# Laying out weights and adapter tables on the host, in a fused four-layer kernel on one Trainium2 core

## The reference, cut to what matters

```
x: [128, 64, 1024] f32
x = x + ssm(x)                      # causal convolution per channel, masked by length, kernel from 64 modes
x = x + einsum('bct,bcd->bdt', x, L1_weights[cond])
x = x + x @ W2.T + bias + (x @ A2[id].T) @ B2[id].T       # W2 [1024,1024], A2 [32,16,1024], B2 [32,1024,16]
x = x + x @ W3.T + 0.5 * (x @ A3[lab]) @ B3.T             # W3 [1024,1024], A3 [5,1024,32], B3 [1024,32]
```

## Time and profile before

| | us |
|---|---|
| median of three runs | 1587.73 |
| lowest, highest | 1584.13, 1589.02 |
| profiled execution, its time | 1586.82 |
| its span, first to last instruction | 1585.1 |
| TensorE busy | 1533.4 (97%) |
| VectorE, ScalarE, GpSimd busy | 992.8, 612.8, 390.3 |

### The profile page before, as it was taken

The page is one execution under the profiler, slowest core; times in us unless marked ns, Lnnn a source line. Parts: engine busy times, 40 slices in busy tenths (PEclk is TensorE's granted clock), DMA queues, the critical chain, the costliest instruction groups (busy, mean ns, idle before and its releaser), DMA issues.

```text
span 1585.1 us, 33854 instructions
## 1 busy us (share of the span) xinstructions
PE 1533.4 (97%) x11213; PEld 1478.3 (93%) x11213; DVE 992.8 (63%) x2010; ACT 612.8 (39%) x1185; POOL 390.3 (25%) x389
## 2 busy tenths in 40 slices
PE   6899989999999999599999999999999999999998
PEld 5778879999999999599999999999999999999998
DVE  7955358888888888545556556455564555655544
ACT  3331245444445545234434334343333433434432
POOL 3551246666666666200000000000000000000000
PEclk9999999999999999699999999999999999999999
DMA  9723156676666666443443534435345353353442
GB/s 242 105 105 102 41 174 235 234 241 234 233 238 238 236 235 218 118 123 107 143 136 101 159 111 138 140 93 166 113 126 149 97 153 125 109 156 106 143 135 73
DMA packets 165103, 243.02 MB, mean 153 GB/s; under 512 B 62113, under 2 KB 118701, under 8 KB 162417
## 3 DMA queue, kind: packets, MB, share of 16 engines
q1 hardware_dynamic: 154844, 208.11, 44.2%
q10 hardware_dynamic: 10230, 34.52, 6.2%
HBM read 167.62 MB, written 74.95 MB: 153 GB/s over the span
## 4 chain that ended last, share of the span: by engine, by line
PE 58%; issue 0%; ACT 0%; DVE 0%; DMA 0%; DVEq 0%
PE ps L1531 23%; PE ps L1532 22%; PE ps L1502 7%; PE ps L1539 2%; PE ps L1541 2%; PE ps L1513 1%; PE ps L1508 0%; DMA x_in<-x_d 0%; ACT a L1303 0%; DVE weights L1399 0%; ACT xa L1305 0%; ACT weights L1315 0%; DVE y_out L1480 0%; ACT xs L1320 0%; DVE y_out L1483 0%
## 5 line engine op out<-in xcount | busy, mean ns | idle before, releaser
L1531 PE MATMUL ps<-weights,xs 128*128 128x256 f32 x1536 | 398.2, 289 | 0.0
L1532 PE MATMUL ps<-weights,xs 128*128 128x256 f32 (+1 forms) x1536 | 389.7, 293 | 0.0
L1531 PE MATMUL ps<-weights,xa 128*128 128x352 f32 (+1 forms) x1152 | 330.9, 314 | 4.4 <-DVE weights L1399 1.3
L1532 PE MATMUL ps<-weights,xa 128*128 128x256 f32 (+1 forms) x1152 | 325.8, 297 | 0.0
L1531 PEld LDWEIGHTS ps<-weights,xs 128*128 128x128 f32 x1536 | 293.1, 191 | 0.0
L1532 PEld LDWEIGHTS ps<-weights,xs 128*128 128x128 f32 x1536 | 292.4, 190 | 0.0
L1277 POOL COPY m_gath<-mix 64x64 f32 x128 | 39.5, 308 | 838.8 <-PE ps L1502 741.0
L1103 PE MATMUL ps<-toep,ut 128*128 128x512 f32 (+2 forms) x1152 | 229.1, 344 | 0.0
L1531 PEld LDWEIGHTS ps<-weights,xa 128*128 128x128 f32 x1152 | 219.1, 190 | 9.7 <-issue 9.7
L1532 PEld LDWEIGHTS ps<-weights,xa 128*128 128x128 f32 x1152 | 218.9, 190 | 0.0
L1303 ACT ACTIVATE a<-ps 128x512 f32<-128x512 f32 x128 | 76.6, 598 | 357.9 <-PE ps L1502 357.9
(11 more groups left out here) (227 smaller groups left out, 2471.1 us busy)
## 6 DMA issues: line engine op xcount, KB each, us to landing
toep_raw<-kern_d SPq DMA_DIRECT2D x64, 512.0 KB, 4.2
xt<-in_x SPq DMA_DIRECT2D x64, 512.0 KB, 5.0
x_d<-xt SPq DMA_DIRECT2D x64, 512.0 KB, 4.4
x_in<-x_d SPq DMA_DIRECT2D x64, 512.0 KB, 5.1
out<-y_out ACTq DMA_DIRECT2D x64, 512.0 KB, 4.3
stack<-b_d SPq DMA_DIRECT2D x130, 128.0 KB, 3.4
tab<-a_d SPq DMA_DIRECT2D x126, 128.0 KB, 2.1
stack<-b_d SPq DMA_DIRECT2D x128, 64.0 KB, 4.2
```

The lines of the kernel that those rows point to most:

```text
L1531: mm(left[0], x_part, left[1], start=first and is_wide, stop=end, skip_group_check=True)
L1532: ins = mm(right[0], x_part, right[1], start=first and is_wide and H_AT[m] > 0, stop=end, skip_group_check=True)
```

## The change

The host hands over seven inputs in the layout in which the products read them (`layouts`): W2 by blocks, W3 transposed, the A2, B2 and A3 tables by partition, B3 transposed, and the bias as a column. In the program:
- The jobs t0 to t7, b3 and la0 to la3 are gone, with their copies, and so are the load and the store of the A2 table: the last stage reads it from the input.
- p3 is split straight from the loaded pieces `p3_raw`, on ScalarE and VectorE, with all eight subtractions in a row in VectorE's list.
- Loads come in rows of 4 KB and more, in fewer issues; P2's block 0 is loaded first. All constants but the identity are made later on GpSimd.
- The bias row: ScalarE scales each piece of p3_raw by the bias in place, GpSimd adds the eight pieces, and two products with ones sum over the partitions.
- The jobs stand in a new order: par behind a3, d1 and d5 ahead of k. The mask, the block splitting, and the stages for b2 are moved in the lists of ScalarE, VectorE and GpSimd.

```diff
-    a2_d = nc.dram_tensor("a2_d", [A2N, P, K8 * R2], F32).ap()
+    a2_d = lora2_a
...
-    ORDER = [(f"t{i}", 1 + i % 3) for i in range(K8)] + [
-        ("d0", 0), ("par", 1), ("d4", 3), ("a3a", 2), ("a3b", 1), ("b2_0", 0), ("b2_1", 3), ("b2_2", 2),
-        ("c", 1), ("row", 0), ("b3", 3), ("k0", 2), ("k1", 1), ("la0", 0), ("la1", 3), ("la2", 2), ("la3", 1),
-        ("d1", 0), ("d5", 3), ("d2", 2), ("d6", 0), ("d3", 1), ("d7", 2), ("b2_3", 3)]
+    ORDER = [
+        ("d0", 0), ("d4", 3), ("a3a", 2), ("a3b", 1), ("par", 0), ("b2_0", 3), ("b2_1", 2), ("b2_2", 1),
+        ("c", 0), ("row", 3), ("d1", 2), ("d5", 1), ("k0", 0), ("k1", 3),
+        ("d2", 2), ("d6", 0), ("d3", 1), ("d7", 2), ("b2_3", 3)]
...
+                sp.dma_start(to[:], w2[i].rearrange("p (c t) -> p c t", c=K8)).then_inc(landed, 16)
+
+            load_p2(p2[0], 0, in_w2[0])
+            for c in range(K8):
+                sp.dma_start(p3_raw[:, c], w3[:, c * T:(c + 1) * T]).then_inc(in_w3[c], 16)
+            load_p2(p2[4], 4, in_w2[4])
+            sp.dma_start(a3raw[:], lora3_a.rearrange("p (c n) -> p c n", c=K8)).then_inc(in_a3, 16)
+            for i in BLOCKS[2:]:
...
+            split = K8 * 3 * P
+            sp.dma_start(b2raw[:], lora2_b[:, 0:split].rearrange("p (c n) -> p c n", c=K8)).then_inc(in_b2, 16)
+            sp.dma_start(b2raw3[:], lora2_b[:, split:].rearrange("p (c n) -> p c n", c=K8)).then_inc(in_b2_3, 16)
+            sp.dma_start(b3_in[B3_ROWS], lora3_b).then_inc(in_b3, 16)
+            sp.wait_ge(consts, CONSTS)
+            sp.dma_start(kern_d[:, T:T + P], zero[:]).then_inc(kern_stored, 16)
...
             sp.wait_ge(job_done, done("k1"))
             for v in range(2):
                 load_p2(p2_late[v], (3, 7)[v], in_late[v])
-            sp.wait_ge(job_free, freed("la3"))
...
-            for i in range(K8):
-                w3_identity(i)
-                if i == 1:
-                    p2_identity(p2[0], 0, in_w2[0])
-                if i == 2:
-                    stage_low(0)
-            for i in BLOCKS[1:]:
+            p2_identity(p2[0], 0, in_w2[0])
+            p3_identity(0)
+            stage_low(0)
+            for i in range(1, K8):
+                p3_identity(i)
+            p2_identity(p2[4], 4, in_w2[4])
+            later_consts()
+            stage_low(1)
+            for i in BLOCKS[2:]:
                 p2_identity(p2[i], i, in_w2[i])
-                if i == 1:
-                    stage_low(1)
...
+            pool.wait_ge(biased, 2)
+            link(tt(waste[:], p3_raw[:, 0, :], p3_raw[:, 1, :], ALU.add))
+            for c in range(2, K8):
+                pool.wait_ge(biased, c + 1)
+                ins = tt(waste[:], waste[:], p3_raw[:, c, :], ALU.add)
+                if c < K8 - 1:
+                    link(ins)
+            ins.then_inc(bias_ready, 1)
+            stage_low(2)
+            stage_low(3)
             pool.wait_ge(part_ready, 1)
+            pool.wait_ge(p3_lo, K8)
             pool.wait_ge(bias_ready, 1)
-            pool.wait_ge(job_done, done("t7"))
             tt(fac_v[:], across(1), steps_of(0), ALU.mult).then_inc(fac_turns, 1)
             tt(fac_t[:], across(0), steps_of(0), ALU.mult).then_inc(fac_decay, 1)
-            stage_low(2)
             pool.wait_ge(fac_exp, 1)
...
             link(tt(fac_u[:], fac_u[:], fac_t[:], ALU.mult))
+            stage_low(4)
             tt(fac_u[:], fac_u[:], across(2), ALU.mult).then_inc(fac_sum, 1)
-            stage_low(3)
             pool.wait_ge(fac_arg, 2)
             tt(fac_v[:], across(1), steps_of(1), ALU.mult).then_inc(fac_turns, 1)
-            stage_low(4)
...
+            stage_high(0)
             for i in range(K8):
-                act.wait_ge(job_done, done(f"t{i}"))
-                copy(p3[:, i, 0, :], target(f"t{i}"), ACT.Copy).then_inc(job_hi, 1)
-                if i == 0:
-                    act.wait_ge(trig_in, 1)
-                    nc.scalar.activation(sin1[:], frac[:], ACT.Sin, scale=TWO_PI).then_inc(trig_out, 1)
-                    nc.scalar.activation(sinh[:], frac[:], ACT.Sin, scale=TWO_PI / 2).then_inc(trig_out, 1)
-                if i == 1:
-                    stage_high(0)
+                act.wait_ge(w3_ready, i + 1)
+                copy(p3[:, i, 0, :], p3_raw[:, i, :], ACT.Copy).then_inc(p3_hi, 1)
             stage_high(1)
-
+            act.wait_ge(trig_in, 1)
+            nc.scalar.activation(sin1[:], frac[:], ACT.Sin, scale=TWO_PI).then_inc(trig_out, 1)
+            nc.scalar.activation(sinh[:], frac[:], ACT.Sin, scale=TWO_PI / 2).then_inc(trig_out, 1)
+
+            act.wait_ge(in_later, 16 * LATER)
+            for i in range(K8):
+                act.wait_ge(p3_lo, i + 1)
+                nc.scalar.activation(p3_raw[:, i, :], p3_raw[:, i, :], ACT.Identity, scale=bias_col[:, i:i + 1]).then_inc(biased, 1)
...
-            act.wait_ge(bias_ready, 1)
+            act.wait_ge(nat_done, 1)
             lower_high(0)
+            upper_high(0)
+            stage_high(2)
+            stage_high(3)
             act.wait_ge(fac_decay, 1)
...
-            stage_high(2)
             act.wait_ge(fac_arg, 2)
             trig(fac_w[:], -TWO_PI, phase[:, 4:5])
-            upper_high(0)
-            stage_high(3)
             act.wait_ge(a3_stored, 16)
             b2_high(0, b2_out)
             stage_high(4)
+            act.wait_ge(b2_stored, 16)
+            b2_high(1, b2_out)
+            stage_high(5)
             act.wait_ge(fac_decay, 2)
             nc.scalar.activation(fac_t[:], fac_t[:], ACT.Exp).then_inc(fac_exp, 1)
             act.wait_ge(fac_arg, 3)
             trig(fac_w[:], -TWO_PI, phase[:, 5:6])
-            for m in (1, 2):
-                act.wait_ge(job_done, done(f"b2_{m}"))
-                act.wait_ge(b2_stored, 16 * m)
-                b2_high(m, b2_out)
-                stage_high(m + 4)
+            act.wait_ge(b2_stored, 32)
+            b2_high(2, b2_out)
+            stage_high(6)
...
+            act.wait_ge(split_const, 4)
...
             def p3_low(i):
-                dve.wait_ge(job_hi, i + 1)
-                tt(p3[:, i, 1, :], target(f"t{i}"), f(p3[:, i, 0, :]), ALU.subtract).then_inc(job_free, 1)
+                dve.wait_ge(p3_hi, i + 1)
+                tt(p3[:, i, 1, :], p3_raw[:, i, :], f(p3[:, i, 0, :]), ALU.subtract).then_inc(p3_lo, 1)
...
+            for i in range(K8):
+                p3_low(i)
             link(tt(e_q[:], e_q[:], e_2k[:], ALU.mult))
...
-            link(ts(mask[:], ramp[:], lens[:], None, ALU.is_lt))
...
-                    link(nc.vector.tensor_tensor_reduce(out=waste[:], in0=w3_raw[:, c, :], in1=b3t[:], scale=1.0, scalar=0.0,
-                                                        op0=ALU.mult, op1=ALU.add, accum_out=bias_p3[:, c:c + 1]))
...
-            link(nc.vector.tensor_copy(part[:], t[:, 0:4 * C].rearrange("p (j h) -> p j h", j=4)))
-            nc.vector.tensor_copy(bias_col[:], t[:, 4 * C:4 * C + K8]).then_inc(part_ready, 1)
-            bias_products(2, K8)
-            nc.vector.memset(waste[:, 0:1], 0.0).then_inc(bias_ready, 1)
+            ts(mask[:], ramp[:], lens[:], None, ALU.is_lt).then_inc(nat_done, 1)
...
+            dve.wait_ge(nat_done, 1)
             lower_low(0)
-            dve.wait_ge(fac_turns, 1)
-            reduced(fac_u[:], fac_v[:], 0)
-            reduced(fac_w[:], fac_v[:], 1)
             upper_low(0)
...
+            dve.wait_ge(job_done, done("par"))
+            nc.vector.tensor_copy(part[:], target("par")[:, 0:4 * C].rearrange("p (j h) -> p j h", j=4)).then_inc(part_ready, 1)
+            dve.wait_ge(part_ready, 1)
+            dve.wait_ge(fac_turns, 1)
+            reduced(fac_u[:], fac_v[:], 0)
+            reduced(fac_w[:], fac_v[:], 1)
...
+            dve.wait_ge(split_const, 4)
+            dve.wait_ge(staged_lo, 7)
+            dve.wait_ge(c_stored, 32)
+            lower_low(1)
+            upper_low(1)
 
...
-            for i in range(4):
-                dve.wait_ge(job_done, done(f"la{i}"))
-                nc.vector.tensor_copy(lora2_out[:, :, 2 * i:2 * i + 2, :].rearrange("p a c r -> p c a r"),
-                                      target(f"la{i}").rearrange("p (c a r) -> p c a r", c=2, a=A2N)).then_inc(job_free, 1)
-
-            dve.wait_ge(staged_lo, 7)
-            dve.wait_ge(c_stored, 32)
-            lower_low(1)
-            upper_low(1)
...
-            for i in range(3):
-                transpose_w3(i)
             for c in range(K8):
-                if c + 3 < K8:
-                    transpose_w3(c + 3)
-                pe.wait_ge(job_free, freed(f"t{c}"))
+                pe.wait_ge(p3_lo, c + 1)
                 pe.wait_ge(staged_lo, 1)
-                ins = chunk_of(target("d0"), 0, c)
+                ins = chunk_of(job("d0"), 0, c)
...
+            parameters()
             for m in range(3):
                 split_job(f"b2_{m}")
...
-            for c in range(K8):
```

(17 more changed lines are left out.)

170 lines of the change are left out of this document (56 added, 114 removed).

## The result

The changed kernel takes **1596.03 us** (median of 7 runs, 1591.16 to 1598.61) against 1587.11 for the kernel before in the same session (7 runs, 1583.09 to 1589.02). The ratio is 1.0057, with a 95% interval of 1.0045 to 1.0068: slower by 7 to 11 us. A second set of runs, in a later session, gave 1.0056 (1.0040 to 1.0073). The forecast was 1595, 1580 to 1602.

A forecast was written before the change was run, and what follows sets the result against it. PE was taken as nearly the bound of the preparation, GpSimd and VectorE just ahead. 156.4 + 43.6 + 1.9 + 12.6 put the first convolution product at 214.5 against 206.8, 7.7 us later: 1595 us, range 1580 to 1602.

The forecast's parts named there:

- TensorE's work removed: Preparation on PE: 10 us gained by the end of A3; without any waits, convolutions reached at 182.3, 24.5 us earlier.
- Deferred constants: GpSimd constants beside the W3 subtractions on VectorE: cost 0 to 1.6 us, taken as 0.
- Bias row: Seven linked GpSimd sums, 29.3 to 47.5, let VectorE do 7 to 14 small operations meanwhile; mask at 54.5.
- Rival A: Small VectorE operations are not held up by the GpSimd sums; mask done at 40, total 1584; chance 0.18.
- First wait: Ahead of b2_0: its low part comes after the late mask, PE idle 9.5 us, start at 64.1.
- Second wait: Ahead of d1: factor chain takes 51 us from 66.5, so d1 starts at 117.5 after 4.7 us idle.
- Rival B: GpSimd and VectorE hardly meet in the new order, factor chain under 45 us; total 1576; chance 0.12.
- Third wait: Ahead of d2: its GpSimd low part stands behind additions awaiting late P2 loads; start at 156.4, idle 11.2 us.
- Clock: After idle stretches PE runs at a lower clock: 1.9 us lost on first and third wait, 1.7 on second.
- Loads: Wider rows land 512 KB blocks 1.3 us apart instead of 1.8; without that the forecast is some 2 us higher.
- Carried over unchanged: Everything behind the first convolution product, including the two long stages (466.7 and 911.6 us), keeps its time.

The follow-up runs named there:

- the three reorderings: Changed kernel with sums behind VectorE's parameter chain, late additions one stage later, second exponential ahead of the b2_1 copy: 1570.08 us, repeat 1570.82.
- the run with the exponential first: Changed kernel with ScalarE's second exponential and sine ahead of the copies that wait for the store of b2_0: 1586.28 us, 1.0024 of the kernel before.
- the run with two sums: Changed kernel with bias pieces 2 to 6 left out, so GpSimd does two of the seven sums: 1583.79 us, 1.0006 of the kernel before.

## Why the prediction was right

The account by steps held, each within 2.2 us of the trace:

| step | predicted | measured |
|---|---|---|
| d0 starts | 11.6 | 12.11 |
| d4 starts | 25.4 | 26.25 |
| A3 ends | 54.0 | 54.8 |
| sums | 29.3 to 47.5 | 30.13 to 47.28 |
| mask done | 54.5 | 55.26 |
| b2_0 starts | 64.1 | 64.87 |
| factor tables start | 66.5 | 67.00 |
| d1 starts (idle) | 117.5 (4.7) | 118.72 (4.70) |
| k starts | 141.0 | 143.06 |
| late loads issued | 147.5 | 149.61 |
| d2 starts (idle) | 156.4 (11.2) | 158.22 (10.93) |
| first convolution product | 214.5 | 215.86 |

- **TensorE's work removed.** 10 us were gained by the end of A3, as said, and nothing that TensorE saved after that reached the end. The text calls the 24.5 us between 182.3 and 206.8 what the edit takes off PE. They are not all work: in the repeat of the three reorderings, where little time is lost to the clock, TensorE is busy for 172.03 us ahead of the start, 15.1 less than before. The other 9 are idle time of the old timeline that the sum leaves out.
- **Deferred constants.** Put at 0, with 1.6 us kept in the range. The last W3 subtraction ended at 22.65 (about 22 said), beside the small constants; the large iota ran behind it, at 22.73, and met two small VectorE operations, which took 0.68 and 2.45 in place of 0.25 each, the second beside the low part of d4.
- **Bias row.** The mechanism was right: with the sums moved behind the chain, 4.5 us came back. Its size: eleven operations during the sums (said 7 to 14), and 2.45 us per sum, not 2.6. What the forecast did not say is that of the 9.58 us of idle time only 5.65 are the hold; 3.93 stay when it is gone, as the sums' own time on GpSimd. Rival A, no hold, is out.
- **First wait.** A detail was missed: par uses the PSUM tile of d0, so it waited for VectorE to split d0 (2.49 us), which the text charged to b2_0. The sum of both, 9.58, is the 9.5 that was said. (The parts given for it there, 3.9, 2.1, 1.05 and 2.4, add up to 9.45, not to 9.6.)
- **Second wait.** The chain from the first table to the end of b2_low(1) took 51.7 us (said 51). The store ahead of the exponential was put at some 5 us; the run with the exponential first gave 5.0 on ScalarE, 3.7 at d1 and 5.35 at the start, since d1 and d5 behind it took 2.4 less (22.01 against 24.41). Rival B needed a chain under 45 us and did not come: the engines still wait for each other in it.
- **Third wait.** Right in place and size. The late loads landed 5.7 us behind their issue (said 6.0). Moving the additions gave 11.9 at the start, against 13.1 (11.2 and 1.9 of clock): d2 came 10.5 sooner and the four jobs took 1.4 less.
- **Clock.** 1.9, 1.7 and 1.9 us were put on the three waits. b2_0 and b2_1 took 24.02 with the first wait and 22.08 in the run with two sums, 1.9 more. d1 and d5 took 24.41 with the wait and 22.01 without, 2.4 more; over the six traces with this wait the excess is 1.5 to 2.9. The four jobs behind the third wait took 45.20 against 43.82, 1.4 more; over six traces 1.4 to 2.8. So the three sizes lie within what one execution differs from another, and that they fit to 0.7 us here is in part luck.
- **Loads.** Pieces landed 1.27 to 1.29 us apart, as taken from the slices in the earlier trace rows. The rule of 512 bytes in the Trainium skill, DMA: Bandwidth & Descriptors, section Specifications, does not hold here as a rule of full rate: rows of 512 bytes load at 291 GB/s and rows of 4 KB at some 410. The cost of narrow loads, put at 2 us, is 3.55.
- **From 214.5 to 215.86.** 0.5 us were missing by the factor tables, 0.7 in the chain and 0.9 in d1 and d5, 2.1 in all at k; from there the late loads came 0.2 sooner than said and the four jobs took 0.5 less.
- **Carried over unchanged.** Both stages behind the start hold the same numbers of products before and after, and no difference by the change shows in them. Over the twelve traces the convolution stage took 461.4 to 463.4 us and the last stage 912.1 to 916.7. The prediction reads 911.6 us for the last stage of before, from the cut at 673.50; the stage takes 916.6. Its sum does not use that length. That the median (1596.03) came so near 1595 is in part luck too: a stage whose length differs by 3.6 us between two executions of one kernel stands behind the start.

That the forecast took the three waits one after another was right too: undone together, they gave 23.6 us.

## What to carry to other kernels

Work taken off the busiest engine is worth only what the engines that feed it can follow: list, for each job, the last operation that it waits for and what is queued ahead of that one, since here the waits in three such queues cost 23.6 us, and one moved loop body turned the sign. Operations that walk SBUF on GpSimd without a pause belong behind a chain of short VectorE operations, not beside it, even if they start 9 us later for it. And an operation that waits for a late load goes behind all work in its queue that does not need the load.
